# Rounding the expert weights on ScalarE, two pieces a step, in place of GpSimd

## The reference, cut to what matters

```python
h  = gelu(xf @ W1[e] + b1[e])                  # first mixture, 8 experts, hidden 256
h1 = jnp.einsum('bsd,edh->bseh', x, w1)        # second mixture, 16 experts, hidden 128
h2 = jnp.einsum('bsd,edh->bseh', x, w2)
hidden = silu(h1) * h2
```

## Time and profile before

| | |
|---|---|
| median of 3 executions | 485.61 us (479.82 to 485.76) |
| the profiled execution | 486.13 us, its span 484.3 us |
| mean granted clock of TensorE | 0.977 |
| attention steps | from 138.5 us to about 281 us of the span |

### The profile page before, as it was taken

How to read it: one execution, slowest core, us unless ns; L and a number is a source line. 1 busy time by engine, 2 the same in 40 slices (tenths; PEclk the granted TensorE clock), 3 DMA queues, 4 the chain that set the end, 5 groups by cost and what they waited for, 6 DMA issues and landing times.

```text
span 484.3 us, 9066 instructions
## 1 busy us (share of the span) xinstructions
PE 435.7 (90%) x2974; PEld 301.7 (62%) x2974; DVE 346.8 (72%) x1090; ACT 283.1 (58%) x676; POOL 174.5 (36%) x304
## 2 busy tenths in 40 slices
PE   2997999999968988979999989999988888989996
PEld 1796777766457887979898944344434534444453
DVE  4178997867777656886988863637667886887864
ACT  3467775732557876857788866765664243343431
POOL 4400001203124563382884333425251354333531
PEclk9999999999989998979999999999999988999999
DMA  7400000000300000012120004112112122133230
GB/s 170 152 2 1 2 0 1 1 2 0 87 3 1 1 2 1 2 43 47 39 50 3 1 3 146 57 40 68 43 54 77 50 72 71 35 93 95 72 124 17
DMA packets 13567, 20.94 MB, mean 43 GB/s; under 512 B 4592, under 2 KB 6384, under 8 KB 13008
## 3 DMA queue, kind: packets, MB, share of 16 engines
q1 hardware_dynamic: 12896, 19.92, 14.5%
q10 hardware_dynamic: 624, 0.43, 0.4%
HBM read 19.62 MB, written 0.72 MB: 42 GB/s over the span
## 4 chain that ended last, share of the span: by engine, by line
PE 64%; DVE 15%; ACT 7%; issue 6%; POOL 4%; DMA 2%; SPq 1%; DVEq 0%; ACTq 0%; POOLq 0%
PE PS L2179 14%; PE PS L1875 7%; PE PS L1913 6%; PE PS L2201 6%; PE PS L2190 5%; PE PS L1934 3%; PE PS L1833 2%; PE PS L2099 2%; PE PS L2111 2%; PE PS L2002 2%; DVE QL L1472 2%; PE PS L2017 2%; PE PS L2049 2%; DVE score_arena L1581 2%; DVE prod L1327 1%
## 5 line engine op out<-in xcount | busy, mean ns | idle before, releaser
L2179 PE MATMUL PS<-YTs,WH 64*128 64x512 f32 x192 | 78.2, 431 | 2.4 <-ACT VV L1067 1.6
L2179 PE MATMUL PS<-YX,WH 64*128 64x512 f32 x192 | 78.3, 431 | 0.0
L735 POOL TENSOR_TENSOR pr<-pr 128x512 f32<-128x512 f32 x38 | 49.2, 1296 | 72.8 <-DVE pr L1634 44.7
L968 ACT ACTIVATE score_arena<-score_arena,nmx 128x128 f32<-128x128 f32 (+1 forms) x128 | 56.9, 447 | 22.2 <-DVE nmx L1581 21.7
L1067 ACT ACTIVATE VV<-PS 128x512 f32<-128x512 f32 x64 | 35.5, 595 | 43.3 <-PE PS L2179 43.3
L2179 PEld LDWEIGHTS PS<-YTs,WH 64*128 64x128 f32 x192 | 35.5, 185 | 31.3 <-ACT VV L1067 12.6
L1747 DVE TENSOR_TENSOR stage<-VV,PS 128x512 f32<-128x512 f32 x64 | 41.7, 683 | 18.1 <-ACT VV L1067 11.3
L1023 ACT ACTIVATE stage<-PS,wk 128x512 f32<-128x512 f32 x64 | 40.8, 684 | 21.4 <-PE PS L2179 21.2
L908 ACT ACTIVATE st_mem<-PS 128x512 f32<-128x512 f32 x72 | 36.9, 609 | 19.4 <-PE PS L1913 19.3
L2111 PE MATMUL PS<-cst,score_arena 128*128 128x128 f32 x192 | 34.1, 288 | 6.1 <-ACT score_arena L968 5.7
L2099 PE MATMUL PS<-YTs,QH 128*128 128x128 f32 (+1 forms) x128 | 39.0, 328 | 0.0
(11 more groups left out here) (277 smaller groups left out, 1126.6 us busy)
## 6 DMA issues: line engine op xcount, KB each, us to landing
QH<-gate_store SPq DMA_DIRECT2D x96, 128.0 KB, 3.0
stage<-in_wexp SPq DMA_DIRECT2D x6, 512.0 KB, 5.9
wk<-in_w SPq DMA_DIRECT2D x1, 1034.0 KB, 8.4
wa<-in_wat SPq DMA_DIRECT2D x1, 768.0 KB, 6.8
cst<-in_consts SPq DMA_DIRECT2D x1, 483.0 KB, 5.3
out<-X SPq DMA_DIRECT2D x14, 32.0 KB, 1.9
wc<-in_w SPq DMA_DIRECT2D x2, 183.5 KB, 5.3
score_arena<-in_wcv SPq DMA_DIRECT2D x2, 144.0 KB, 5.5
```

Source lines behind the costliest of these rows:

```text
L735: nc.gpsimd.tensor_tensor(acc[:, c % 2], acc[:, c % 2], weighted[:, u % 2], ALU.add).then_inc(acc_added, 1)
L968: ins = nc.scalar.activation(PR[:, s % 3, cols], MS[:, s % 3, cols], ACT.Exp, bias=nmx[:, s % 3, qt:qt + 1], scale=-1.0, accum_out=rsum[:, ...
L2179: ins = mm(PS[:, banks[i], :], w[hs, m, tiles[i] * P:(tiles[i] + 1) * P], ys[i][hs, cs], start=(k == 0), stop=(k == 2))
```

## The change

The rounded copies leave GpSimd. ScalarE makes them with an activation `Copy`, two pieces of 128 x 256 at the end of each of the steps 26 to 29 (part 0), 37 to 40 (part 1) and 48 to 51 (part 2), after a wait for the load of that part. GpSimd's `split_stage` keeps only the eight subtractions, each behind a wait for its rounded piece, and its steps move from 25, 33 and 41 to 30, 41 and 52. The loads are issued as before, each by the last subtraction of the part before it.

```diff
-SPLIT_AT = (25, 33, 41)
+SPLIT_AT = (30, 41, 52)
+HIGH_AT = (26, 37, 48)
...
             def split_stage(m):
                 pool.wait_ge(stage_loaded, 32 * (m + 1))
                 for at in range(0, NEXP, PIECE):
-                    step(nc.gpsimd.tensor_copy(WH[:, m, at:at + PIECE], stage[:, at:at + PIECE]))
-                settle()
-                for at in range(0, NEXP, PIECE):
+                    pool.wait_ge(high_ready, m * (NEXP // PIECE) + at // PIECE + 1)
                     nc.gpsimd.tensor_tensor(WL[:, m, at:at + PIECE], stage[:, at:at + PIECE], WH[:, m, at:at + PIECE].bitcast(F32),
                                             ALU.subtract).then_inc(stage_split, 1)
...
                     for name in attention_fills(s):
                         if name[0] in ("q", "v"):
                             project(name)
+                for m in range(3):
+                    if 0 <= s - HIGH_AT[m] < 4:
+                        act.wait_ge(stage_loaded, 32 * (m + 1))
+                        for at in range(2 * PIECE * (s - HIGH_AT[m]), 2 * PIECE * (s - HIGH_AT[m] + 1), PIECE):
+                            nc.scalar.activation(WH[:, m, at:at + PIECE], stage[:, at:at + PIECE], ACT.Copy).then_inc(high_ready, 1)
```

More of the change, by code:

```diff
@@ L430, in hybrid_kernel @@
         stage_split = sem("stage_split")
+        high_ready = sem("high_ready")
         misc_filled = sem("misc_filled")
```

## The result

The changed kernel takes 496.08 us (median of four runs, 491.79 to 500.34); the kernel before, over four runs beside it, 482.72 (479.75 to 485.76). It is 1.023, with a 95% interval of 1.017 to 1.029: a loss of 11.3 us, clear of noise; whether it is more than two per cent is not settled. In a second session, beside 17 runs of the kernel before (median 483.40), it took 496.29 (491.80 to 499.99), 1.024 [1.016, 1.032].

What follows compares the result with a forecast made beforehand. Attention steps were taken as bound by TensorE, ScalarE and VectorE handing work on; 5.1 + 2.0 + 0.4 + 1.0 - 1.0 - 0.5 = +7.0 us on 486.1 gave 493.1, or 492.6 against the median, range 487 to 499.

Steps and rivals of the forecast that it cites:

- The wait: End of step 48: ScalarE stands still for the load of part 2, and TensorE loses 5.1 us (4.6 to 5.7).
- I take 6.0: Load of part 2: 6.0 us from the last subtraction of part 1 to landing, from earlier loads of 5.6 and 6.3.
- The clock after the stall: Behind TensorE's new gap: granted clock falls to 0.50, costing 2.0 us, between 0 and 3.4.
- The copies: Rounded copies on ScalarE: 0.4 us for parts 0 and 1, 1.0 for steps 49 to 51, 0.62 within step 48's wait.
- The relief: VectorE in attention runs faster without GpSimd's casts beside it: -1.0 us together, between -0.3 and -2.5.
- the norms: Layer norm of step 29: two or three VectorE operations get faster without casts beside them, 0.5 us.
- the old gap: TensorE's 3.0 us gap before 211.44 shrinks to about 2 us, its slow stretch perhaps halved: -0.5 us (0 to -3.4).
- they now lie beside other norms and the gate work of step 54, and take perhaps 0.3 back: GpSimd's 24 subtractions, only moved, slow VectorE at their new places and cost perhaps 0.3 us of the relief.
- the first: Rival: load of part 2 is in time and the relief decides, 479.7 us, or 482 with part of it; chance 0.08.
- the small terms: What the first rival leaves without the wait: at most -2.5 us for VectorE and -3.4 for the slow stretch.
- ScalarE as bound: Rival: copies fully on the chain (6.8 us), plus the wait and slow clock, 500 us; chance 0.10.
- The wait alone: Rival: the wait is there but nothing else is lost, +2.9 us, 488.5 us; chance 0.10.

Runs made afterwards that it cites:

- the kernel with its own load: Changed kernel with part 2 loaded into memory of its own, right behind the load of part 1: 486.62 us, ratio 1.0035 to the kernel before.

## Why the prediction was right, and where it was short

*The wait.* Right in every link, and one link too short. The last subtraction was predicted 0.8 us ahead of the moment when ScalarE wants part 2, and was 0.9 ahead (251.45 and 252.35). The copies took 0.63 us up to the exponential, predicted 0.6. The term that was mis-sized is "I take 6.0" for the load: it took 258.70 - 251.45 = 7.25, and 7.35 to 7.5 in three other traces with this wait. I had read the end of the traffic off the windows (5.6 and 6.3 us) and taken it for the landing. The bulk of the traffic ended at about 257.2, 5.8 us after, as predicted, and the last of it before 257.6; the engine that waited went on 1.1 to 1.5 us after that. Nobody waited for a load in the trace of before, so it did not show this piece, and a bound for it was owed.

*The clock after the stall.* Predicted 2.0. Held against the kernel with its own load, which has the same copies and the same third split, step 50 took 6.45 more, about the wait of 6.35, and steps 51 to 53 took 1.7 more: 1.8 for the clock. The size is right for a wrong reason. I had given the slow stretch before 3.4 us by the earlier trace rows, but the windows that those rows leave out are at 0.50 too, so it lasted 6.8 us:

```profile
216.00:217.70 1.70, 1.70 (x10) 1.70 (x9) 1.21 (x4) 1.05 (x5) 0.58 (x1) 0.50 0.98 265
217.70:219.40 1.70, 1.70 (x9) 1.70 (x10) 0.68 (x5) 0.00 (x0) 0.00 (x0) 0.51 1.02 227
```

The new one has 6.2 us of work in it, of which 1.8 and not 3.1 reached the masks. What the term left out is the stretch from 277.6, 5.5 us in the execution of 500.34. Whether the other executions above 491.8 have it, no trace shows. Its cause isn't settled: a gap of TensorE of 1.19 us ends at 277.22 ahead of it, but 0.95 at the same place in the trace of the rows, and 1.55 in the experiment with copies two steps earlier, had no such stretch behind them.

*The copies.* Predicted 0.4 + 1.0 + 0.6 in step 48 = 2.0; alone they cost 2.1, though with more in the first two parts (1.1) than I gave them.

*The relief.* The burst of step 38 gained 0.8, as predicted. The gap before the old slow stretch shrank from 3.00 to 2.21, predicted 2. Steps 29 to 33 gained 1.68, the norms (predicted 0.5) and the old gap (predicted 0.5) in one, but most of that is luck: the stretch at 0.50 behind the gap was 3.4 us in this trace (211.9 to 215.3) and 6.8 in the one before. Behind the same gap of 2.2 us there was none with the own load, 3.4 us in the execution of 500.34, 7.0 with the second split in step 40 and 10.4 with the own load and the split in step 57. Where it was 7.0, much as before, steps 29 to 34 gained 0.3. But "they now lie beside other norms and the gate work of step 54, and take perhaps 0.3 back" was wrong by a factor of four: 1.33. I had priced a subtraction like a cast, though the trace of before has one operation of step 30 beside a subtraction, which took less than half of that in the changed kernel with GpSimd idle; first before, then changed:

```profile
209.94 0.95 DVE L1408 TENSOR_TENSOR Y<-Y 128x256 f32<-128x256 f32 x1
```

```profile
210.06 0.41 DVE L1413 TENSOR_TENSOR Y<-Y 128x256 f32<-128x256 f32 x1
```

*The sum.* With the sizes that the traces gave: wait 5.1 + 1.25, clock 1.8, copies outside step 48 2.1 - 0.6, third split 1.33, relief and old gap -0.82 - 1.68, together +8.5; the masks show 9.8 from mask 0 to mask 63. The rest lies in steps 1, 2 and 23, in steps 39 to 42 and in step 50, each a few tenths. Without the wait and its clock, and with slow stretches alike (relief -0.8 - 0.3), the same terms give 2.1 + 1.33 - 1.1 = +2.3, inside the 0 to 3.4 us of the kernel with its own load. The trace is of the fastest execution; what makes the others slower is shown for the one of 500.34 only. For the rest only the mean granted clocks speak (0.960 and 0.970 beside 0.978), so that part of the loss stays open.

*The rivals.* The load was not in time, so the first is out; its own sum for the small terms was wrong too, since with no wait these are no gain (1.0035 [1.0000, 1.0070]). ScalarE as bound is out: 2.1 us for 24 copies and not 6.8. "The wait alone" is out by the slow clock behind the gap.

## What to carry to other kernels

When a transfer is issued by the last reader of its buffer, moving that reader moves the landing: write down when the reader is done, when the next user wants the data and how long an engine that waits stands still, and not only how long bytes move. Taking work off an idle engine gives back only what others lose beside it, so look at what its remaining work will lie beside once it has moved. A wait of 6.35 us cost 8.1 here in the traces, of which 1.8 because TensorE came back from it at half its clock, and 7 to 10 by the ratios. And compare single traces only after finding their stretches at half clock: behind the same gap they lasted from nothing to 10.4 us.

## What the runs showed of the hardware

- The two engines' neighbourhood has a price by the kind of operation. A 128 x 32 operation of VectorE with two inputs in SBUF took 0.19 us alone, 0.31 to 0.43 beside GpSimd's one-input casts, and mostly 0.39 to 0.77 beside its two-input subtractions; a 128 x 256 multiplication 0.42, 0.61 and 0.95. A reduction with one input stayed at 0.19 in the same bursts, but a one-input rounding copy of 128 x 256 took 0.29 alone, 0.37 beside casts and 0.70 beside subtractions. GpSimd itself lost little: eight subtractions took 6.17 us beside the norm and 5.6 elsewhere. The Trainium skill, page "SBUF — State Buffer", section "Who interferes with whom", calls the shared ports an exclusive lock. That VectorE waits for nearly a whole subtraction (about 0.7 us) fits; that GpSimd lost about 0.5 us in all beside 4.3 us of VectorE's busy time does not show a lock held in the other direction.
- A load of 1 MB in two halves moved the bulk of its bytes within 5.8 us of the subtraction that released its issue and the last of them within 6.2, and released a waiting engine 1.1 to 1.5 us later. The Trainium skill, page "DMA: Bandwidth & Descriptors", section "Anatomy of one DMA — SWDGE (gpsimd) path", puts most of a DMA's fixed time between the last byte and the semaphore; the 1.1 to 1.5 us agree, though this load was issued by SyncE.
- Behind gaps of TensorE of 2.5 to 6.3 us its granted clock was 0.50 for some time, and the longer gap did not have the longer slow stretch behind it: 2.51 was followed by 3.4 us, 3.00 by 6.8, 2.60 by 9.9, and 6.26 by 6.2 after the return. Nor does the gap's length settle it: eight traces with the same gap of 2.2 us near 211 had 0, 3.4, 7.0 or 10.4 us behind it.
